# Another order of blocks within one turn of the attention loop

## Chip, cores and metric

The kernel runs on one core of one Trainium2 chip. The metric is the device time of one execution in microseconds; lower is better. Three runs of the kernel before gave 1092.05, 1092.52 and 1094.72.

## What is computed

The input is x, 16 batches of 128 channels by 512 positions, and a context of the same shape. One layer of cross-attention is followed by one layer with a mixture of experts:

```
x = x + xattn(layernorm(x), ctx)      # per batch: q, k, v = 128x128 projections over channels,
                                      # rotary embedding on q and k, 8 heads of 16 channels,
                                      # softmax over 512 positions, output projection
x = x + moe(layernorm(x))             # 2048 tokens of width 512, 32 experts of inner width 192,
                                      # router logits, the best 8 experts, softmax over these 8,
                                      # silu(gate) * up, weighted, down projection, sum
```

## The kernel before

The program is written by hand for each engine, with semaphores between them. It has two parts: the attention with the routing (up to about 534 us of the trace), and a loop over tiles of tokens of one expert (to the end). Only the first part matters here.

The attention is a software pipeline over the 16 batches. In turn `it` the engines work on several batches at different stages: `bl` = it+4 (first normalisation), `bq` = it+3 (projections and rotary embedding of queries and keys), `b1` = it+1 (maxima of the scores, values), `b2` = it (scores, exponentials, averages), `bo` = it-1 (end of the averages, division by the sums, output projection, residual sum), `br` = it-2 (second normalisation, tokens transposed, logits, routing). `batch_turns` (line 274) runs the turns -5 to 19; turns 0 to 14 follow the general order that the change touches, turn 15 and the ones after it have orders of their own.

The names of the work in one general turn:

- TensorE: `s(n)` makes two blocks of scores, n and n+1, side by side (48 or 49 rows each, line 1822); 32 blocks a turn. `m(n)` makes the block of scores for the n-th maximum, also two matmuls side by side (line 1845); 16 a turn. `pv(k)` is the k-th average, eight matmuls in columns of 32, float32 (line 1834); it needs four exponentials. `project` and `project_turned` are the projections of queries and keys and of their turned halves (lines 1520 to 1527, float32; "qr" for the queries and "kr" for the keys), `values` line 1537, `max_rows` the transposes of the maxima (line 1581, first half "mt0", second half "mt1"), `tokens_transposed` line 1586 ("xt"), `logits` line 1606, `output` line 1542, `counts_of` line 1615.
- VectorE: `maximum` (line 1086) reads a block of `m`; `rope` (line 1092) reads a projection; `reciprocal` (line 1120); `highest` and `highest_index` (lines 1149 to 1154) search the best experts in the logits; `choose` (line 1160) compares expert numbers; `weights`, `residual` (line 1231), `read_counts`, `places`, and two statistics (line 1111) before the next turn's first maximum.
- ScalarE: `exponential` (line 813) reads a block of `s`; `read_o` reads the finished averages with their sums out of PSUM, `max_row` the transposed maxima, `high_of_qk` makes the float16 high part of the embedded queries (0) and keys (1), `normal_x`, `normal_x2` normalise, `high_of_x2`, `read_xt`, `read_v`, `turned_half`, `exponentials_of_top`.
- GpSimd: the small steps of both normalisations, products and sums of the rotary embedding (lines 720 and 734), `scale_o` (line 727), low parts (line 606), and the scatter of the routing rows (line 627). Its order is left as it is.
- SyncE issues all other DMAs in an order of its own, which is left as it is: among them the store of the sums (`den_store`), loads of the stacked queries and keys, the store of a row of maxima (`store_mrow`), `store_stack` and the token store.

What sets the order: each engine works strictly in the order of its own `turn` function. PSUM is shared by two rings. The ring of two double banks (`in_v_banks`) is used in turn by m0, the projections, m1 to m8, the logits, m9 to m15, the output and the counts; the ring of three single banks (`in_s_banks`) by the transposed maxima (mt1), s0 to s7, qr, s8 to s11, kr, s12 to s15, xt, s16 to s19, the values, s20 to s25, mt0, s26 to s31. `bank_is_free` (line 296) makes TensorE wait until the tenant two (or three) places back was read. The orders in these two rings are left as they are. Exponentials go to a ring of eight buffers, so e(n) waits for pv(n//4 - 2); the averages have one bank, so pv0 and pv4 wait for `read_o`.

Of the kernel before, what the change touches and what calls it, by code (L numbers as in the profile page):

```python
# [98 lines left out]
def xattn_moe(nc, x, ctx, proj_w, proj_b, value_b, out_w, gate_w, expert_w, const_f, const_h, const_m, out):  # L99
# [26 lines left out]
    with ctxs:  # L126
# [675 lines left out]
        def _(act):  # L802
# [12 lines left out]
            def read_o(b, g):  # L815
                act.wait_ge(pv_mm, b.count(8, 4 * g + 4))

                need(act, on_done, b.count(2, g - 3))
                need(act, den_out, b.count(16, -16))
                copy(o_raw[:, b.slot(2), g, :], ps_o).then_inc(o_read, 1)  # L820

            def max_row(b, half):
                act.wait_ge(mt_mm, b.count(2, half + 1))
                need(act, mrow_in[(b + -1).slot(2)][half], (b + -1).rounds(2, 16, 16))
                copy(mrow[:, half, :], bank(f"mt{half}")[0:16, 0:P], -1.0 / MSCALE).then_inc(mrow_done, 1)
# [15 lines left out]
            def turn(it):  # L841
                bl, bq, b1, b2, bo, br = it + 4, it + 3, it + 1, it, it + -1, it + -2
# [18 lines left out]
                def exponentials_of_top():  # L861
                    act.wait_ge(ntop_done, br.count(1, 1))
                    need(act, rows_done, br.count(3, 0))
                    nc.scalar.activation(ex[:, :], top[:, :], ACT.Exp, bias=ntop[:, 0:1], scale=1.0 / WSCALE, accum_out=exs[:, 0:1]).then_inc(ex_done, 1)

                def normal_x():
                    act.wait_ge(shift1, bl.count(1, 1))
                    need(act, turn_mm, bl.count(2, -1))
                    nc.scalar.activation(xn[:, :], x_in[:, bl.slot(2), :], ACT.Identity, bias=shift[:, 0:1], scale=rstd[:, 0:1]).then_inc(xn_done, 1)


                def exponentials(first, n):
                    if b2.live():
                        for i in range(first, first + n):
                            exponential(b2, i)
# [48 lines left out]
                    return  # L924
                if b2.live():
                    max_row(b2, 1)
                exponentials(0, 6)
                if bo.live():
                    read_o(bo, 1)
                if br.live():  # L930
                    normal_x2(br)
                exponentials(6, 1)
                if br.live():
                    high_of_x2(br)
                exponentials(7, 1)
                if bq.live():
                    turned_half(bq, 0)
                exponentials(8, 4)
# [2 lines left out]
                exponentials(12, 4)  # L941
                if br.live():
                    read_xt()
                exponentials(16, 2)
                if b2.live():
                    read_o(b2, 0)
                exponentials(18, 2)
                if b1.live():
                    read_v(b1)
                exponentials(20, 3)  # L950
                if bq.live():
                    high_of_qk(bq, 0)
                exponentials(23, 1)
                if bq.live():
                    high_of_qk(bq, 1)
                exponentials(24, 2)
                if b1.live():
                    max_row(b1, 0)
                exponentials(26, 3)
                if bl.live():  # L960
                    normal_x()
                exponentials(29, 1)
                if br.live():
                    exponentials_of_top()
                exponentials(30, 2)

            batch_turns(act, turn)

# [533 lines left out]
        def _(pe):  # L1502
# [115 lines left out]
            def turn(it):  # L1618
                bq, b1, b2, bo, br = it + 3, it + 1, it, it + -1, it + -2

                def s(first):
                    if b2.live():
                        for n in (first, first + 1):
                            bank_is_free(pe, it, f"s{n}")
                            scores(b2, n)

                def m(n):
                    if b1.live():
                        bank_is_free(pe, it, f"m{n}")
                        scores_for_maxima(b1, n)  # L1630
# [112 lines left out]
                elif b1.live():  # L1743
                    bank_is_free(pe, it, "qk")
                    constants_into("qk", 2)
                s(6)
                if bq.live():
                    bank_is_free(pe, it, "qr")
                    project_turned(bq, 0)
                elif b1.live():  # L1750
                    bank_is_free(pe, it, "qr")
                    constants_into("qr", 1)
                m(1)
                pv(0)
                s(8)
                m(2)
# [9 lines left out]
                m(4)  # L1766
                s(12)
                pv(2)
                m(5)
                s(14)  # L1770
                if br.live():
                    bank_is_free(pe, it, "xt")
                    tokens_transposed(br)
                m(6)
                m(7)
                s(16)
                pv(3)
                s(18)
                m(8)
# [11 lines left out]
                m(11)  # L1791
                s(24)
                m(12)
                if b1.live():
                    bank_is_free(pe, it, "mt0")
                    max_rows(b1, 0)
                pv(5)
                m(13)
                s(26)
                s(28)  # L1800
                m(14)
                pv(6)
                s(30)
                m(15)
                if bo.live():
                    bank_is_free(pe, it, "y")
                    output(bo)
# [193 lines left out]
```

## Time and profile before

| | |
|---|---|
| median of 3 runs | 1092.52 us (1092.05 to 1094.72) |
| the profiled execution | 1093.14 us, span 1091.3 us |
| granted TensorE clock, mean | 0.966 |
| busy: TensorE, VectorE, ScalarE, GpSimd | 999.5, 701.7, 771.1, 747.1 us |
| 256 maxima on VectorE | 303.9 us, 1222 ns each |
| 512 exponentials on ScalarE | 278.6 us, 603 ns each |

Busy time is that in which an engine executes; it says nothing of why it is idle at other times. The ends of matmuls are modelled, and neighbouring instructions overlap a little at both ends, so the distance between two starts is the better measure of what a step costs. In the rows of a timeline the bracket at the end is idle time just before the instruction and what ended it.

### The profile page before, as it was taken

Reading aid. Unit: us, or ns where it says so; the run is one execution under the profiler, and the core shown is the slowest. Engines: PE = TensorE matmul, PEld = TensorE weight load, DVE = VectorE, ACT = ScalarE, POOL = GpSimd, SP = SyncE. Lnnn points to the kernel's source line nnn. Section 1 sums busy time; section 2 is a strip of 40 time slices with the busy share of each in tenths; the row PEclk is TensorE's granted clock in tenths of the full one; section 3 lists DMA queues with packets and bytes.
Section 4 is the critical chain, followed back from the end, with each engine's and each line's share of the span. In section 5 each row is a group of like instructions: output and inputs, shape, how many; then the busy total and the mean of one; then the engine's idle time right before and its main releaser. Section 6 shows DMA issues by size and latency. Waiting matters only on the chain.

```text
span 1091.3 us, 29745 instructions
## 1 busy us (share of the span) xinstructions
PE 999.5 (92%) x7228; PEld 478.8 (44%) x7229; DVE 701.7 (64%) x1349; ACT 771.1 (71%) x1791; POOL 747.1 (68%) x675
## 2 busy tenths in 40 slices
PE   6689999999999999993499999999999999999995
PEld 2222222222222222231366666666666666666662
DVE  4778899999999988886354555453553554553521
ACT  2278888888888887781367667767677776677673
POOL 5434577777777774457467777777777777777774
PEclk9599999999999999996699999999999999999998
DMA  5524444444344333320588789898789898889673
GB/s 169 159 70 123 139 130 129 126 132 120 118 126 130 119 109 115 98 96 22 173 217 215 212 204 241 216 216 219 198 201 238 215 223 213 218 194 233 119 144 58
DMA packets 88948, 174.56 MB, mean 160 GB/s; under 512 B 23754, under 2 KB 40698, under 8 KB 84786
## 3 DMA queue, kind: packets, MB, share of 16 engines
q0 software_dynamic: 38144, 74.53, 32.0%
q1 hardware_dynamic: 50736, 99.26, 28.5%
q8 instruction: 28, 0.46, 0.2%
q14 instruction: 36, 0.29, 0.1%
q10 hardware_dynamic: 4, 0.02, 0.0%
HBM read 117.26 MB, written 61.58 MB: 164 GB/s over the span
## 4 chain that ended last, share of the span: by engine, by line
PE 41%; issue 4%; DVEq 3%; DVE 2%; DMA 1%; ACTq 1%; ACT 1%; POOL 1%; POOLq 0%; SPq 0%
PE ps L1873 22%; PE ps L1881 5%; PE ps L1899 2%; PE ps L1901 2%; PE ps L1903 2%; PE ps L1902 2%; PE ps L1900 2%; DVEq L374 2%; DVE w_lo L1463 1%; PE ps L1889 1%; DVE w_hi L1458 1%; PE ps L1891 1%; PE ps L1890 1%; ACTq L374 1%; POOL expert_rows L627 0%
## 5 line engine op out<-in xcount | busy, mean ns | idle before, releaser
L1086 DVE TENSOR_REDUCE mx<-ps 128x2 f32<-128x1024 f32 x256 | 303.9, 1222 | 33.9 <-PE ps L1845 29.9
L1873 PE MATMUL ps<-w_hi,o_raw 128*128 x1184 | 313.5, 327 | 0.0
L787 POOL DMA_INDIRECT out<-v,s_idx x148 | 248.2, 1677 | 94.1 <-ACT g_idx L803 41.5
L813 ACT ACTIVATE pr<-ps 128x512 f32<-128x512 f32 x512 | 278.6, 603 | 45.8 <-PE ps L1822 44.6
L766 POOL DMA_INDIRECT pr<-normalised_tokens,g_idx x150 | 163.0, 1087 | 51.8 <-issue 21.7
L1873 PE MATMUL ps<-w_lo,o_raw 128*128 x592 | 193.4, 327 | 0.0
L803 ACT ACTIVATE o_raw<-ps 128x1024 f16<-128x1024 f16 (+1 forms) x180 | 171.9, 955 | 1.3 <-PE ps L1881 1.1
L627 POOL DMA_INDIRECT expert_rows<-rows,rowi x128 | 129.1, 1008 | 38.3 <-issue 37.3
L1873 PEld LDWEIGHTS ps<-w_hi,o_raw 128*128 128x128 f16 x1184 | 116.1, 98 | 84.5 <-issue 0.7
L1475 DVE SCALAR_TENSOR_TENSOR rope_b<-rope_a,stacks,ps 128x192 f32<-128x192 f32 x148 | 60.6, 410 | 142.8 <-ACT rope_a L973 103.9
L1834 PE MATMUL ps<-pr,v 128*32 128x512 f32 x1024 | 136.4, 605 | 0.4 <-issue 0.3
L1845 PE MATMUL ps<-stacks 48*128 48x512 f16 x512 | 104.5, 394 | 21.2 <-DVE mx L1086 18.1
L1822 PE MATMUL ps<-stacks 49*128 49x512 f16 x512 | 112.3, 386 | 12.5 <-ACT pr L813 11.9
L1881 PE MATMUL ps<-ch,pr 128*128 128x128 f16 x1184 | 91.2, 220 | 23.6 <-DMA pr<-normalised_tokens,stacks 22.0
L1480 DVE TENSOR_TENSOR rope_s<-rope_b,rope_s 128x128 f16<-128x128 f32 x148 | 43.0, 291 | 107.3 <-ACT rope_s L803 107.3
L803 ACT ACTIVATE v<-ps 128x512 f32<-128x512 f32 x164 | 96.7, 590 | 2.1 <-PE ps L1537 1.7
L1881 PEld LDWEIGHTS ps<-ch,pr 128*128 128x128 f16 x1184 | 78.2, 98 | 44.3 <-issue 26.1
L1463 DVE SCALAR_TENSOR_TENSOR w_lo<-stage,w_hi x155 | 95.7, 680 | 0.1
L803 ACT ACTIVATE rope_s<-rope_b 128x192 f16<-128x192 f32 x148 | 54.3, 367 | 51.9 <-DVE rope_b L1475 51.7
L803 ACT ACTIVATE x<-ps 128x384 f16<-128x384 f16 x148 | 72.7, 491 | 21.6 <-PE ps L1891 20.9
L1822 PEld LDWEIGHTS ps<-stacks 49*128 49x128 f16 x512 | 30.2, 93 | 123.1 <-ACT pr L813 74.8
L1458 DVE TENSOR_SCALAR w_hi<-stage x62 | 50.1, 849 | 44.6 <-PE ps L1903 35.4
(177 smaller groups left out, 1476.8 us busy)
## 6 DMA issues: line engine op xcount, KB each, us to landing
stage<-in_expert_w SPq DMA_DIRECT2D x32, 1280.0 KB
stacks<-qk_parts SPq DMA_DIRECT2D x128, 96.0 KB
w_lo<-in_x SPq DMA_DIRECT2D x32, 256.0 KB, 2.9
w_lo<-in_ctx SPq DMA_DIRECT2D x32, 256.0 KB, 5.7
qk_parts<-qk SPq DMA_DIRECT2D x32, 256.0 KB
qk_parts<-qk SPq DMA_DIRECT2D x32, 128.0 KB
out<-x SPq DMA_DIRECT2D x16, 256.0 KB, 4.8
normalised_tokens<-x2s SPq DMA_DIRECT2D x16, 256.0 KB, 2.5
```

Source lines behind the costliest of these rows:

```text
L627: nc.gpsimd.indirect_dma_start(rows_d, bass.IndirectOffsetOnAxis(rowi[:, b.slot(2), k:k + 1], 0), rows[:, b.slot(2), k, :], None).then_inc ...
L766: nc.gpsimd.indirect_dma_start(xg[:, r, :], None, tok_d, bass.IndirectOffsetOnAxis(indices, 0)).then_inc(gathered[r], 16)
L787: nc.gpsimd.indirect_dma_start(out_rows, bass.IndirectOffsetOnAxis(s_idx[:, s.slot(4), 0:1], 0), y_sb[:, s.slot(4), :], None, bounds_check ...
L803: copy = lambda o, i, s=1.0: nc.scalar.activation(o, i, ACT.Copy, scale=s)
L813: nc.scalar.activation(pr[:, n % 8, :], bank(f"s{n}"), ACT.Exp, scale=DH ** -0.5).then_inc(exp_done, 1)
L1086: V.tensor_reduce(mx[:, b.slot(2), at:at + 3:2, tile], bank(f"m{n}"), AXX, ALU.max).then_inc(mx_done, 1)
L1463: lo = V.scalar_tensor_tensor(w_lo[:, bass.ds(at_slot + at, LO_PIECE)], stage[:, bass.ds(at_src + at, LO_PIECE)], WSCALE, w_hi[:, bass.ds( ...
L1822: mm(bank(f"s{n}"), k_st[rows_of, b.slot(2), p, sc * P:(sc + 1) * P], q_st[rows_of, b.slot(2), p, :], start=True, stop=True).then_inc(s2_m ...
L1834: last = mm(ps_o[2 * DH * i:2 * DH * (i + 1), :], v1[:, b.slot(2), k % NSC, head, :], pr[:, (4 * k + i) % 8, :], start=(k % NSC == 0), sto ...
L1845: last = mm(bank(f"m{n}")[:, side, :], q_st[rows_of, b.slot(2), p, i * P:(i + 1) * P], k_st[rows_of, b.slot(2), p, :], start=True, stop=True)
L1873: last = mm(ps[:, s.slot(2), 0:2 * INTER], xt[:, s.slot(2), at:at + P], w[:, cols], start=(m == 0), stop=(m == 3 * KT - 1))
L1881: last = nc.tensor.transpose(ps[:, 2 + s.slot(2), :].bitcast(F16)[:, n * P:(n + 1) * P], xg[:, s.slot(GROUP), n * P:(n + 1) * P], ident)
```

## The change

Only the general turn is touched, on TensorE and on ScalarE. No instruction is added or taken away.

```diff
 (ScalarE, turn)
-                exponentials(0, 6)
+                exponentials(0, 4)
                 if bo.live():
                     read_o(bo, 1)
+                exponentials(4, 2)
                 if br.live():
                     normal_x2(br)
-                exponentials(6, 1)
                 if br.live():
                     high_of_x2(br)
-                exponentials(7, 1)
+                exponentials(6, 2)
                 if bq.live():
                     turned_half(bq, 0)
...
-                exponentials(16, 2)
+                exponentials(16, 4)
                 if b2.live():
                     read_o(b2, 0)
-                exponentials(18, 2)
                 if b1.live():
                     read_v(b1)
-                exponentials(20, 3)
+                exponentials(20, 2)
                 if bq.live():
                     high_of_qk(bq, 0)
-                exponentials(23, 1)
+                exponentials(22, 4)
+                if br.live():
+                    exponentials_of_top()
+                if b1.live():
+                    max_row(b1, 0)
+                exponentials(26, 4)
+                if bl.live():
+                    normal_x()
+                exponentials(30, 1)
                 if bq.live():
                     high_of_qk(bq, 1)
-                exponentials(24, 2)
-                if b1.live():
-                    max_row(b1, 0)
-                exponentials(26, 3)
-                if bl.live():
-                    normal_x()
-                exponentials(29, 1)
-                if br.live():
-                    exponentials_of_top()
-                exponentials(30, 2)
+                exponentials(31, 1)
 (TensorE, turn)
                 s(6)
+                m(1)
                 if bq.live():
                     bank_is_free(pe, it, "qr")
                     project_turned(bq, 0)
...
-                m(1)
                 pv(0)
...
                 pv(2)
+                s(14)
                 m(5)
-                s(14)
+                m(6)
                 if br.live():
                     bank_is_free(pe, it, "xt")
                     tokens_transposed(br)
-                m(6)
+                s(16)
                 m(7)
-                s(16)
                 pv(3)
...
                 m(12)
+                pv(5)
                 if b1.live():
                     bank_is_free(pe, it, "mt0")
                     max_rows(b1, 0)
-                pv(5)
+                s(26)
                 m(13)
-                s(26)
                 s(28)
                 m(14)
                 pv(6)
+                m(15)
                 s(30)
-                m(15)
                 if bo.live():
                     bank_is_free(pe, it, "y")
                     output(bo)
```

## Rows read from the trace of the kernel before

**Rows 1.** Stretches: start:end, us, busy of each engine, PEclk, DMA share, GB/s
```profile
105.99:133.71 27.72, 26.27 (x188) 7.97 (x186) 24.44 (x33) 23.86 (x47) 15.62 (x20) 1.00 0.45 136
...
216.82:244.53 27.71, 26.29 (x194) 8.03 (x190) 25.44 (x39) 23.84 (x47) 21.40 (x24) 1.00 0.44 134
```
**Rows 2.** Timeline, TensorE, the turn from 216.82: start, us, engine, line, waits
```profile
219.42 0.39 PE L1822 MATMUL ps<-stacks 49*128 49x512 f16 x1 [0.25 <-ACT pr L813]
...
230.73 0.39 PE L1845 MATMUL ps<-stacks 48*128 48x512 f16 x2 [0.23 <-DVE mx L1086]
...
237.41 0.39 PE L1845 MATMUL ps<-stacks 48*128 48x512 f16 x2 [0.23 <-DVE mx L1086]
...
240.23 0.39 PE L1822 MATMUL ps<-stacks 49*128 49x512 f16 x1 [0.47 <-ACT pr L813]
```
**Rows 3.** The same timeline, steps of TensorE without a wait
```profile
219.74 1.12 PE L1520 MATMUL ps<-xn,pw 128*128 128x512 f32 x2
...
221.65 0.39 PE L1822 MATMUL ps<-stacks 49*128 49x512 f16 x2
221.97 1.12 PE L1525 MATMUL ps<-xn,pw 128*128 128x512 f32 x2
223.03 0.39 PE L1845 MATMUL ps<-stacks 48*128 48x512 f16 x2
223.35 1.06 PE L1834 MATMUL ps<-pr,v 128*32 128x512 f32 x8
224.35 0.39 PE L1822 MATMUL ps<-stacks 49*128 49x512 f16 x2
...
229.02 0.39 PE L1845 MATMUL ps<-stacks 48*128 48x512 f16 x2
229.24 0.38 PE L1822 MATMUL ps<-stacks 49*128 49x512 f16 x2
...
237.73 0.28 PE L1581 MATMUL ps<-ident,mx 128*16 128x128 f32 x1
237.94 1.06 PE L1834 MATMUL ps<-pr,v 128*32 128x512 f32 x8
...
242.30 1.98 PE L1542 MATMUL ps<-o_n,ow 128*128 128x512 f32 x4
```
**Rows 4.** Timeline, VectorE, the same turn
```profile
220.97 1.23 DVE L1086 TENSOR_REDUCE mx<-ps 128x2 f32<-128x1024 f32 x1
...
223.46 1.23 DVE L1086 TENSOR_REDUCE mx<-ps 128x2 f32<-128x1024 f32 x1
225.00 1.23 DVE L1086 TENSOR_REDUCE mx<-ps 128x2 f32<-128x1024 f32 x1 [0.31 <-PE ps L1845]
...
229.45 4.69 DVE L1086 TENSOR_REDUCE mx<-ps 128x2 f32<-128x1024 f32 x4
234.40 0.20 DVE L1149 MAX8 top<-ps 128x8 f32<-128x32 f32 x1 [0.26 <-PE ps L1606]
...
236.14 2.35 DVE L1086 TENSOR_REDUCE mx<-ps 128x2 f32<-128x1024 f32 x2
...
242.41 1.23 DVE L1086 TENSOR_REDUCE mx<-ps 128x2 f32<-128x1024 f32 x1 [0.31 <-PE ps L1845]
243.55 0.41 DVE L1160 TENSOR_TENSOR chosen<-cf,topi 128x256 f16<-128x256 f32 x1
...
244.41 0.68 DVE L1231 TENSOR_TENSOR x<-ps,w_lo 128x512 f32<-128x512 f32 x1
```
**Rows 5.** Timeline, ScalarE, the same turn
```profile
222.93 0.61 ACT L803 ACTIVATE x2s<-xn 128x512 f16<-128x512 f32 x1
...
239.58 1.57 ACT L813 ACTIVATE pr<-ps 128x512 f32<-128x512 f32 x3 [0.70 <-PE ps L1822]
```
**Rows 6.** Timeline, GpSimd, the same turn
```profile
223.62 1.17 POOL L606 TENSOR_TENSOR x2s<-xn,x2s 128x512 f16<-128x512 f32 x1 [0.39 <-ACT x2s L803]
...
241.54 1.16 POOL L606 TENSOR_TENSOR qk<-rope_s,qk 128x512 f16<-128x512 f32 x1
```

## The prediction

> **What bounds the kernel now.** I first read busy time in stretches [rows 1], one stretch per turn of the attention loop. From 105.99 to 466.28 thirteen turns take 27.71 us each on average (the first and the fifth are shown), at a granted TensorE clock of 1.00. In the fifth TensorE is busy for 26.3 us, VectorE in 25.4, ScalarE in 23.8, GpSimd in 21. No engine is full, so the turn is set by a chain that hops between engines. The change touches nothing after the last turn.
>
> Next the timeline of one turn, from 216.82; all offsets below are us after that start. I call the pairs of score blocks s0 to s30, the blocks for the maxima m0 to m15, their readings on VectorE M0 to M15, the exponentials e0 to e31, the averages pv0 to pv7. TensorE stands still in five places, of which four are shown [rows 2]: before s5 (offset 2.60, for e2), m7 (13.91, for M5), m12 (20.59, for M10) and s29 (23.41, for e26); m10 waits for the search of the top experts as m7 and m12 do. Pairs otherwise follow at 0.22 [rows 3]; so s5 is late by 0.63, m7, m10 and m12 by 0.4 each, s29 by 0.85: 2.7 us, which leaves 25.0 us of TensorE's own work. VectorE stands still before M2 (offset 8.18, where M1's start plus 1.14 is 7.78) and in the same way before M3, M4, the search and M15 [rows 4], 2.0 us together: its work is 25.7 us. So 2.0 us a turn is the most that any order can win (26 us in all).
>
> Which waits matter? I follow the chain back from the turn's end. The residual sum (27.59) starts 2.00 after M15 (25.59), and M15 starts 0.42 after m15 (25.17). From the residual sum to the next M0 is 4.27 of VectorE's work in a row (27.59 to 31.86). The block m15 goes back over pv6, m14 and s29 to e26, whose start is 0.65 before s29 [rows 2, 5], then to s26, m12, M10 and so on to M5 and m4. Of the waits, s5 and the first block of the turn are off it: the project block that follows s5 only has to be there before M0 is through.
>
> **The change, part by part.** Durations are taken from the same rows: from a pair to a pair 0.22 to 0.23; from a pair to another kind 0.32; an average 1.00; one turned projection 1.06 when a pair follows [rows 3]; a maximum 0.42 after its block (229.02 to 229.45), the next piece of VectorE 1.14 later (242.41 to 243.55); the block that needs its bank 1.28 after the reading's start (229.45 to 230.73, 236.14 to 237.41) [rows 2, 4].
>
> 1. *m1 ahead of the turned projection of the queries (qr).* Before: s6 at 4.83, qr 5.15, m1 6.21, pv0 6.53. The block m1 needs the bank that M0 reads (M0 at 4.15), so it can't start before 5.43, 0.38 later than TensorE would get there. Behind it stand qr (5.75) and pv0. The join qr to pv0 isn't in the trace: it lies between half of the two projections in a row (1.91/2 = 0.95) and 1.06 [rows 3]. I take 1.00, pv0 at 6.75: 0.22 later than now. M1 itself was ready at 6.64 on both sides (M0, two rope sums, then M1), so the earlier m1 wins nothing on VectorE.
> The Trainium skill (TensorEngine Tiling, Key Properties) says that a change of tiling mode drains TensorE; by it qr to pv0 still pays a drain and would cost the 1.06. That would put 0.06 on every turn. The trace agrees that a change of kind costs 0.10 (0.32 against 0.22).
>
> 2. *s14 ahead of m5, and m6 ahead of the token transposes.* All between pv0 and pv2 keeps its order, so pv2 is at 11.42 (was 11.20). Then s14 12.42 and m5 12.65 (was 12.20 [rows 3]). M5 starts at 13.07 (was 12.63): this is 0.22 from part 1 and 0.22 from the s14 put in front. The moved transposes hide: m7 waits for M5 till 14.35 anyhow, and s17, which now waits for e15 till about 13.98, hides in the same wait. From m7 to M10 nothing changes, but this stretch has two rails. TensorE's rail (m7, pv3, s18, values, logits) is at +0.44; VectorE's was idle for 0.35 before the search (17.58, [rows 4]) and is so no gate. m7 to logits is now 0.23 shorter, as s16 has moved ahead of m7 into the wait; so the logits and the search behind them are at +0.21, 17.79. So M10 is at 19.53, m12 at 20.80 (was 20.59): +0.21.
>
> 3. *pv5 ahead of the transpose of the first maxima; s26 ahead of m13.* Before m12, transpose, pv5, m13, s26: s26 at 22.34, 1.75 after m12. Now m12, pv5 (0.31), transpose (1.00), s26 (0.21): 1.52 after m12, so s26 at 22.32. The join pv5 to transpose isn't shown; it lies between 0.90 and 1.06 (an average's 1.00 less or plus a change of kind), I take 1.00. The reading of this transpose (ScalarE, about 22.4 to 22.7) now ends just when e26 can start (22.74). So s29 comes at 23.39, m14 at 23.61, as before. The +0.21 is made good here. The row of maxima leaves SyncE's queue 0.6 later; it is not needed before the next turn's s0, over 3 us on.
>
> 4. *m15 ahead of s30.* pv6 at 23.92, m15 at 24.92 instead of 25.17, M15 at 25.34 instead of 25.59. But the residual sum needs the output block too. That starts at 25.46 (was 25.48) and the residual needs 2.03 from there (242.30 to 244.41 is 2.11 with M15 as the gate; 1.98 is its own length [rows 3, 4]). So the residual starts at 27.49, not at 27.34. Won: 0.10.
>
> 5. *ScalarE's order.* The reading of the averages moves ahead of e4 and e5; it starts 0.95 earlier, as pv7 was long done. The store of the sums gets ahead, but the reciprocal stands behind M4 on VectorE and had no wait: nothing won. e4 is needed only at 4.83 minus 0.65. The high part of the second normalisation now directly follows it and waits for its own input some 0.2; e6 shifts from 5.63 to about 6.35, needed by s8 at 7.75: hidden. The high part of the keys moves from 20.33 to 26.05, behind e30. GpSimd's low part of them starts 0.69 after it (222.93 to 223.62 [rows 5, 6]), at 26.7 instead of 24.72, and queued behind it are two row scatters, two stack stores and the token store. GpSimd is done about 30.4, the next turn wants it at 31.0: hidden, with 0.6 to spare. The top exponentials go 3 us earlier; VectorE, which takes them up behind the comparison (26.73), had no wait there.
>
> Sum: the next M0 at 27.49 + 4.27 = 31.76, and the next turn's start at 27.69; M0 is then at offset 4.07, 0.08 earlier than I began with. As m1 and all behind it hang on M0, the steady turn is 27.69 - 0.08 = 27.61, against 27.70: **0.09 us shorter**. Thirteen steady turns [rows 1] give 1.2 us; the first two, with parts missing, nothing I can price. The profiled execution took 1093.14 (span 1091.3, 1.84 around it): 1091.9 by the sum. The median of before is 0.62 below that execution, so the forecast is 1092.5 - 1.2 = **1091.3 us**. The open joins (-0.05/+0.06, -0.10/+0.06) and latencies read to 0.03 make -0.18/+0.15 a turn: 1089.0 to 1093.5 on its own.
>
> **Rivals.**
> *The joins are cheap and the output is not the gate* (27%). If qr to pv0 costs 0.90, the transpose after pv5 0.90, and the residual sum follows M15, a turn is 27.3 to 27.4: 0.35 less, 4.6 us, 1087.9. For it: VectorE's rail has the room. Against: the output block is measured at 1.98.
> *TensorE loses more in the first half than it gets back* (15%). m1's wait for M0 and the s14 in front of m5 put 0.44 on M5. If e26 is held up by the late reading of the maxima's transpose (margin 0.07), part 3 gives back nothing: a turn is 27.70 + 0.21 = 27.9, 1095.3. It decides as soon as that reading ends after 22.8.
> *GpSimd is in the way of the comparison* (8%). The comparison (243.55, both inputs in SBUF, 0.41 long [rows 4]) now starts about 0.26 before GpSimd's low part of the keys, which lasts 1.16 [rows 6]; the two never overlap in this trace. Should the low part start first and hold the comparison back, it would wait till 27.8 instead of 26.4, the residual sum starts at about 28.7, 1.2 late, in some 11 turns: 13 us, 1105. It decides if M15 is 0.26 late against s30. The Trainium skill (SBUF — State Buffer, Who interferes with whom) speaks for it: a VectorE instruction with two SBUF inputs contends with a GpSimd instruction that reads SBUF, and the first to start wins; no row here shows it.
> *The orders don't matter* since each engine waits for the same chain: 1092.5; it lies inside the forecast's range.
>
> **The chances.** Forecast 50%, the others 27, 15, 8. A change under 0.3% (3.3 us) is no change to this measurement. The forecast's range is nearly all within that; the first rival is mostly beyond; of the second only half. Faster 0.32, the same 0.46, slower 0.22. The range 1086.0 to 1097.0 leaves out the third rival and tails.
>
> **What would show it.** A steady turn of 27.61 between transposes of the second maxima; m1 waiting for M0 at 5.4; M5 0.4 later in the turn; waits at m7, m12 and s29 still there; M15 earlier, the residual sum not; GpSimd's low part right behind the comparison's start. A turn under 27.45 or over 27.85 makes me wrong; a comparison or a product of chosen and place that starts late while GpSimd is busy names the third rival.

## The result, and the profile after

The changed kernel takes 1100.20 us (median of 6 runs, 1098.25 to 1103.26), the kernel before 1092.71 beside it (6 runs, 1091.71 to 1094.72): a ratio of 1.0068, 95% interval [1.0055, 1.0081]. The forecast was 1091.3 with a range up to 1097.0, so it missed both the sign and the range. The profiled execution took 1098.71 (span 1096.9, granted clock 0.967).

The loss lies in the attention loop. Between transposes of the second maxima the turns of before were 29.37, 26.97, 27.72, and then 27.70 each (one 27.85). After the change they are 28.73, 27.04, 27.39, 28.25, 28.25, 28.51, 27.98, 28.24, 28.24, 28.25, 30.22, 27.74, 29.10, 27.56, 27.37. The last of these transposes starts at 472.32 instead of 466.28: 6.0 us later, of 5.6 in the span.

The same view as [rows 1], two turns of after:

```profile
217.62:245.60 27.98, 26.63 (x193) 8.30 (x189) 25.72 (x39) 24.25 (x47) 20.84 (x23) 1.00 0.42 126
245.60:273.84 28.24, 26.62 (x192) 8.30 (x189) 25.98 (x39) 24.25 (x47) 21.09 (x24) 1.00 0.43 125
```

In the second of them VectorE is busy 0.54 us longer than in [rows 1] (25.98 against 25.44), with the same instructions. One line grouped by form tells which. First before, then after; the columns are the duration in ns (min/median/max) and the first and last start:

```profile
L1173 DVE TENSOR_SCALAR rows<-ex,exr x16: 233/235/341, 133.3 to 509.2; 128x8 f32<-128x8 f32 x16
```
```profile
L1171 DVE TENSOR_SCALAR rows<-ex,exr x16: 233/936/943, 131.9 to 515.3; 128x8 f32<-128x8 f32 x16
```

This scales the 8 routing weights of each token: 128 by 8 numbers, 0.23 us of work, that now takes 0.94. The timeline of VectorE at the end of the turn from 245.60, the counterpart of the last two of [rows 4]:

```profile
272.65 0.41 DVE L1158 TENSOR_TENSOR chosen<-cf,topi 128x256 f16<-128x256 f32 x1
272.99 0.15 DVE L1170 RECIPROCAL exr<-exs 128x1 f32<-128x1 f32 x1
273.18 0.94 DVE L1171 TENSOR_SCALAR rows<-ex,exr 128x8 f32<-128x8 f32 x1
274.03 0.22 DVE L1172 TENSOR_SCALAR rows<-zero,cf 128x16 uint32<-128x16 f32 x1
274.17 0.68 DVE L1229 TENSOR_TENSOR x<-ps,w_lo 128x512 f32<-128x512 f32 x1
```

GpSimd and ScalarE at the same time (compare [rows 6], where the low part of the keys ran at 241.54, well before the comparison at 243.55):

```profile
270.13 1.28 POOL L727 TENSOR_TENSOR o_n<-o_raw,rcb 128x512 f32<-128x512 f32 x1
272.91 1.17 POOL L606 TENSOR_TENSOR qk<-rope_s,qk 128x512 f16<-128x512 f32 x1 [1.51 <-ACT qk L803]
...
272.22 0.62 ACT L803 ACTIVATE qk<-rope_s 128x512 f16<-128x512 f32 x1
```

ScalarE's high part of the keys (272.22) releases GpSimd's low part at 272.91. VectorE's comparison had started 0.26 earlier and runs undisturbed; the scaling comes in the middle and ends at 274.12, when GpSimd's instruction (272.91 + 1.17 = 274.08) is through. The residual sum stands behind it.

In the turn from 330.33 (30.22 us) it was worse. VectorE, GpSimd and TensorE there:

```profile
353.85 3.62 DVE L1084 TENSOR_REDUCE mx<-ps 128x2 f32<-128x1024 f32 x3
357.38 1.15 DVE L1158 TENSOR_TENSOR chosen<-cf,topi 128x256 f16<-128x256 f32 x1
358.46 0.15 DVE L1170 RECIPROCAL exr<-exs 128x1 f32<-128x1 f32 x1
358.65 0.93 DVE L1171 TENSOR_SCALAR rows<-ex,exr 128x8 f32<-128x8 f32 x1
...
360.35 0.69 DVE L1229 TENSOR_TENSOR x<-ps,w_lo 128x512 f32<-128x512 f32 x1 [0.64 <-PE ps L1540]
...
354.64 1.28 POOL L727 TENSOR_TENSOR o_n<-o_raw,rcb 128x512 f32<-128x512 f32 x1 [2.94 <-DMA rcb<-reciprocals]
355.88 1.16 POOL L606 TENSOR_TENSOR qk<-rope_s,qk 128x512 f16<-128x512 f32 x1
356.99 1.26 POOL L727 TENSOR_TENSOR o_n<-o_raw,rcb 128x512 f32<-128x512 f32 x1
358.21 1.34 POOL L606 TENSOR_TENSOR qk<-rope_s,qk 128x512 f16<-128x512 f32 x1
...
358.36 1.95 PE L1540 MATMUL ps<-o_n,ow 128*128 128x512 f32 x4 [1.94 <-DVE mx L1084]
```

The load of the reciprocals came 2.94 us late, GpSimd's chain with it, and now the comparison itself is held (1.15 instead of 0.41) and the output block waits 1.94. The bracket puts that down to VectorE's maximum, whose last one ended at 357.47 at the latest (353.85 + 3.62), 0.9 before; what ended it is GpSimd's second product (356.99 + 1.26 = 358.25). The residual sum (360.35) waits 0.64 for the output, so in this turn the late products set the length and the held instructions of VectorE do not. Each kernel has one traced execution; this one took 1098.71, 1.5 under its kernel's median.

### The profile page after: what moved, and what is told of

It reads as the page before. It is cut to its first block, busy times and chain, and to the rows that moved or that the text cites. A ratio compares the mean times of both kernels' runs of the same rounds, so it can differ in the third digit from the quotient of the medians.

```text
span 1096.9 us, 29745 instructions
## 1 busy us (share of the span) xinstructions
PE 1004.5 (92%) x7228; PEld 482.1 (44%) x7229; DVE 707.6 (65%) x1349; ACT 776.4 (71%) x1791; POOL 746.1 (68%) x675
## 4 chain that ended last, share of the span: by engine, by line
PE 42%; issue 3%; DVEq 2%; DVE 1%; DMA 1%; ACTq 1%; POOL 1%; ACT 0%; POOLq 0%; SPq 0%
PE ps L1871 23%; PE ps L1879 5%; PE ps L1897 2%; PE ps L1899 2%; PE ps L1901 2%; PE ps L1900 2%; PE ps L1898 2%; DVEq L374 1%; PE ps L1887 1%; PE ps L1889 1%; PE ps L1888 1%; DVE w_lo L1461 1%; DVE w_hi L1456 1%; ACTq L374 0%; DMA out<-v,s_idx 0%
## 5 line engine op out<-in xcount | busy, mean ns | idle before, releaser
L1820 PE MATMUL ps<-stacks 49*128 49x512 f16 x512 | 119.9, 388 | 10.3 <-ACT pr L813 9.3
L1820 PEld LDWEIGHTS ps<-stacks 49*128 49x128 f16 x512 | 32.1, 93 | 129.6 <-ACT pr L813 65.8
L1871 PEld LDWEIGHTS ps<-w_lo,o_raw 128*128 128x128 f16 x592 | 58.0, 98 | 45.9 <-issue 0.3
```

The costliest lines, as they stand in the source:

```text
L1820: mm(bank(f"s{n}"), k_st[rows_of, b.slot(2), p, sc * P:(sc + 1) * P], q_st[rows_of, b.slot(2), p, :], start=True, stop=True).then_inc(s2_m ...
L1871: last = mm(ps[:, s.slot(2), 0:2 * INTER], xt[:, s.slot(2), at:at + P], w[:, cols], start=(m == 0), stop=(m == 3 * KT - 1))
```

## The experiments

In the first three batches (e, n) the kernel before took 1125 to 1136 us; in the last two (p, s, q) 1093, as in the forecast. A ratio is against before in the same batch and on the same chip. The e runs were on two chips (e1 to e4, e5 to e8), and the n runs came later on the second of these: the kernel before took 1125.35 there beside e5 to e8 and 1135.69 beside n1 to n4. The p, s and q runs share a third chip. In the expectations theory A is that GpSimd's late low part of the keys, holding VectorE, is the cause; the rival, by whatever letter, is that TensorE's order has a price of its own.

**Moving the high part of the keys, both ways.** On the changed kernel e1 puts it back (as do e5, q1); its edit is shown. On the kernel before e2 moves it alone, from behind e23 to behind e30:

```diff
-                exponentials(22, 4)
+                exponentials(22, 2)
+                if bq.live():
+                    high_of_qk(bq, 1)
+                exponentials(24, 2)
...
-                exponentials(30, 1)
-                if bq.live():
-                    high_of_qk(bq, 1)
-                exponentials(31, 1)
+                exponentials(30, 2)
```

> The changed kernel with one edit: ScalarE's high part of the keys back behind e23, where it was before. Theory A (port): GpSimd's low part of the keys holds VectorE's scaling of the routing weights (0.23 us before, 0.94 us after); with the high part early the low part ends before the comparison, the scaling is 0.23 again, and a steady turn falls from 28.25 to 27.6 to 27.75 us (28.25 less 0.52 that the held scaling puts behind the output's end, or less 0.71 if the output is no gate). Over 12 turns 6 to 8 us: 1091.5 to 1094 us, level with the kernel before (1092.7). Theory B (TensorE's order): the loss comes from m1 waiting for M0 and s14 ahead of m5; the turn stays at 28.0 or more and the time at 1097 or more.

> The kernel before with one edit: the high part of the keys behind e30. Theory A: e30 starts at offset 25.7, so the high part at 26.2 and GpSimd's low part at 26.8 to 28.0; VectorE's scaling at 27.26 is held till 28.0, it lasts about 0.95 us, the residual sum starts 0.7 late, the turn is 28.3 to 28.4, and the time 1092.7 + 12 x 0.7 = 1100 to 1102 us. Theory B: the kernel before keeps its turn of 27.70 and its time of 1092.7, since GpSimd has 0.6 us to spare.

e1: 1136.49 against 1125.48, 1.0100 [1.0065, 1.0134]; e2: 1127.32, 1.0009 [0.9988, 1.0030]. The scaling did as theory A says: 0.23 in e1, 0.94 in e2. VectorE and GpSimd in e2:

```profile
248.83 0.94 DVE L1173 TENSOR_SCALAR rows<-ex,exr 128x8 f32<-128x8 f32 x1
249.82 0.68 DVE L1231 TENSOR_TENSOR x<-ps,w_lo 128x512 f32<-128x512 f32 x1
...
248.46 1.29 POOL L606 TENSOR_TENSOR qk<-rope_s,qk 128x512 f16<-128x512 f32 x1 [2.15 <-ACT qk L803]
```

Four turns of e2 are 28.14 to 28.16, 0.45 over the 27.70 of before; four others are 29.6, and no trace of the kernel before was taken on this chip, so the 0.45 is a comparison across chips. In the whole time it doesn't show: theory A asked for 7 to 9 us more, e2 is 1.8 above before (interval -1.4 to +3.4). And e1's time did not come back: its turns are mostly 30.2 to 31.3 on this chip. The held instruction stood; that it was the loss did not, there.

**The scaling ahead of the last maximum** (on the changed kernel):

```diff
-                maxima(9, 7)
+                maxima(9, 6)
                 if br.live():
+                    weights(br, link)
+                maxima(15, 1)
+                if br.live():
                     choose(br)
-                    weights(br, link)
```

> The changed kernel with one edit on VectorE: the routing weights ahead of the last maximum, behind M14, where GpSimd waits for ScalarE. Their exponentials are ready by offset 22.4 in the changed order. Theory A: scaling 0.23 us, the comparison directly before the residual sum, GpSimd's low part meets nothing that needs its port (the comparison starts 0.2 us before it); a steady turn is 27.6 to 27.75, the time 1091.5 to 1094 us. Theory B: 1097 or more.

1148.65, 1.0213 [1.0178, 1.0248]. Slower yet: the scaling is out of GpSimd's way and the comparison is put in it.

```profile
289.09 0.23 DVE L1171 TENSOR_SCALAR rows<-ex,exr 128x8 f32<-128x8 f32 x1
289.23 0.23 DVE L1172 TENSOR_SCALAR rows<-zero,cf 128x16 uint32<-128x16 f32 x1
289.36 1.22 DVE L1084 TENSOR_REDUCE mx<-ps 128x2 f32<-128x1024 f32 x1
290.50 1.35 DVE L1158 TENSOR_TENSOR chosen<-cf,topi 128x256 f16<-128x256 f32 x1
...
290.42 1.15 POOL L606 TENSOR_TENSOR qk<-rope_s,qk 128x512 f16<-128x512 f32 x1 [5.01 <-ACT qk L803]
```

**GpSimd's low part in halves** (changed kernel; two subtractions of 256 columns):

```diff
+                if w == 1:
+                    sub(qk[:, 2 * w + LO, 0:T // 2], rope_s[:, w, 0:T // 2], ...)
+                    sub(qk[:, 2 * w + LO, T // 2:T], rope_s[:, w, T // 2:T], ...)
+                    return
```

> The changed kernel with one edit on GpSimd: the low part of the keys as two subtractions of 256 columns instead of one of 512. Theory A says that VectorE's scaling waits for the end of the GpSimd instruction that runs when it wants to start, so it now waits for the first half only: it lasts 0.4 to 0.6 us instead of 0.94, and about 0.4 us a turn come back. If instead the two share the port's bandwidth, or GpSimd's being busy at all is what counts, it stays at 0.9 and more.

1139.31, 1.0113 [1.0068, 1.0157]. The scaling takes 0.45: it waits for the end of the GpSimd instruction that is under way, not for the row of them. The next VectorE instruction (L1176, 0.23 elsewhere) then takes 0.72, to 255.04, when the second half is through (253.70 + 1.31 = 255.01).

```profile
253.44 0.41 DVE L1162 TENSOR_TENSOR chosen<-cf,topi 128x256 f16<-128x256 f32 x1
...
253.96 0.45 DVE L1175 TENSOR_SCALAR rows<-ex,exr 128x8 f32<-128x8 f32 x1
254.32 0.72 DVE L1176 TENSOR_SCALAR rows<-zero,cf 128x16 uint32<-128x16 f32 x1
254.96 0.68 DVE L1233 TENSOR_TENSOR x<-ps,w_lo 128x512 f32<-128x512 f32 x1
...
253.70 1.31 POOL L606 TENSOR_TENSOR qk<-rope_s,qk 128x256 f16<-128x256 f32 x2 [3.96 <-ACT qk L807]
```

From the comparison's start to the residual sum's it is 1.52, as in the changed kernel (272.65 to 274.17): the 0.4 us a turn that the expectation hoped for did not come back, since each half held one instruction.

**TensorE's order with ScalarE as before** (e4, e6), **e1 again** (e5), **e1 with the reciprocal of the sums one maximum earlier** (e8):

```diff
 (e4, e6: the changed TensorE turn on the kernel before; e8, VectorE:)
-                maxima(1, 4)
+                maxima(1, 3)
                 if bo.live():
                     reciprocal(bo)
-                maxima(5, 4)
+                maxima(4, 5)
```

> TensorE's order of the changed kernel with ScalarE's order of the kernel before. Theory A: no held scaling, so 27.6 to 27.9 a turn, 1091 to 1095 us; the transpose of the maxima is read by ScalarE where it was before, behind e25. Theory B: this is where the loss is: a turn of 28.2 and 1098 us or more.

> TensorE's order of the changed kernel with ScalarE's order of the kernel before, once more. Theory A, where the transposes are read 0.66 us after their start: scaling 0.23 us, 27.6 to 27.9 a turn, total within 3 us of the kernel before. Theory B: 28.2 a turn and 6 us more.

> The same edit as in the first run (high part of the keys back behind e23), once more. There TensorE's transposes of the tokens ended 1.2 us later than in the two traces the study began with, in every turn, and so did the logits in half of them; the kernel before was 1125 us there. Theory A (port), on a chip where the transposes take 0.66 us from start to reading: scaling 0.23 us, a steady turn of 27.6 to 27.75 us, total within 2 us of the kernel before. Theory B (TensorE's order itself loses): 28.0 or more a turn and at least 4 us more than the kernel before. If the chip is again one where before needs 1125 us: turns of 30 us as in the first run.

> The changed kernel with the high part of the keys behind e23 and, on VectorE, the reciprocal behind M3 instead of M4. The reciprocals then come back from memory about 1.2 us earlier, so GpSimd's products no longer wait for them (0.8 us a turn in the changed kernel's trace, 2.9 and 1.8 in two turns that became 2.0 and 0.9 us longer). Theory A: as e5, without those two long turns: 27.5 to 27.7 a turn, 0 to 3 us below the kernel before. Theory B: 28.0 or more.

e4 1139.05, 1.0123 [1.0096, 1.0151]; e6 1137.61, 1.0112 [1.0068, 1.0156]; e5 1138.82, 1.0113 [1.0081, 1.0145]; e8 1134.75, 1.0086 [1.0061, 1.0111]. So on these chips TensorE's order costs over 1% with ScalarE's left alone. That is a second cost, beside theory A. e8 takes away the waits for the reciprocals in the steady turns, which stay at 30.2: those waits aren't it.

**Both kernels again, part 2 alone, and part 2 undone** (n3 on the kernel before; n4 undoes it in e1):

```diff
 (n3; n4 is the reverse, in e1)
                 pv(2)
+                s(14)
                 m(5)
-                s(14)
+                m(6)
                 if br.live():
                     bank_is_free(pe, it, "xt")
                     tokens_transposed(br)
-                m(6)
-                m(7)
                 s(16)
+                m(7)
```

> The changed kernel, nothing edited, to have its trace on the same chip as the other experiments. In eight runs the kernel before needed 1125 us, and in TensorE's new order the transposes of the tokens were ready 1.2 us late in every turn from turn 3 on. Theory C (dense spots): where many short TensorE instructions stand together (8 transposes with 8 weight loads, 12 logits with 12 loads) this chip runs late, and the new order, with m5, m6 and the transposes behind one another, makes that worse. It expects 1.2 us late transposes here too and, with the held scaling (0.94 us) on top, a time of 1138 to 1145 us. Theory A alone (port) expects it 6 us above the experiment with the high part of the keys early (1136 to 1139): 1142 to 1145. If it is at 1138 or less, the held scaling is hidden by the late transposes on this chip.

> The kernel before, nothing edited, for its trace on this chip. It must come out at the same time as the kernel before beside it (ratio 1.00). Theory C: its transposes are read at the usual 1.07 us after their start (ScalarE's own pace) in turns 3 to 12, the logits are late in some turns, turns are 27.7 to 29 us, and the stage between the attention and the loop of the experts is longer than in the first trace (39 us there).

> The kernel before with one edit on TensorE: s14, m5, m6, transposes, s16, m7 instead of m5, s14, transposes, m6, m7, s16. Theory C: the transposes come 1.2 us late in every turn from turn 3 on, a steady turn is 29.5 to 30.5 us and the time 1135 us or more on a chip where before is at 1125; on a chip where before is at 1093, no such delay and 1092 to 1095. The rival (the delay comes from m1 standing ahead of the projection, or from pv5): this kernel stays at the time of before.

> The changed kernel with the high part of the keys behind e23 and with this one part of TensorE's order (s14, m5, m6, transposes, s16, m7) put back as before. Theory C: no late transposes, a steady turn of 27.5 to 28.5 us, the time level with before or up to 4 us below. The rival: turns of 30 us and 1135 us or more as in the experiment that leaves this part in.

Before was at 1135.69 in this batch. n1 1155.14, 1.0191 [1.0150, 1.0232], nearly three times the first result's loss; n2 1137.04, 1.0013 [0.9986, 1.0041]; n3 1142.55, 1.0041 [1.0016, 1.0066]; n4 1142.52, 1.0071 [1.0038, 1.0104]. The traces show where the extra goes. TensorE, VectorE and ScalarE in n1:

```profile
240.09 0.62 PE L1584 MATMUL ps<-ch,x2s 128*128 128x128 f16 x8
245.09 0.46 PE L1604 MATMUL ps<-gws,x2t 128*128 128x32 f16 x12
247.75 0.39 PE L1843 MATMUL ps<-stacks 48*128 48x512 f16 x2 [1.66 <-issue]
...
247.13 0.20 DVE L1147 MAX8 top<-ps 128x8 f32<-128x32 f32 x1 [1.70 <-PE ps L1604]
...
242.00 1.02 ACT L803 ACTIVATE x2t<-ps 128x1024 f16<-128x1024 f16 x1 [1.15 <-PE ps L1584]
```

The transposes of tokens started at 240.09 are read at 242.00, 1.91 later, and the logits (245.09) at 247.13, 2.04 later. In the first result's trace of the same kernel these are 0.66 and 0.60. In n2, the kernel before, they are mostly 1.07 and between 0.61 and 1.46 for the first eleven batches of tokens, against 1.07 and 0.60 in the forecast's trace, and its turns are mostly 29.0. The granted clock is 1.00 in the stretch from 170 to 260 of n1. So on these chips the results of the short matmuls reach their readers late, the more so in the new order. Part 2, which stood under suspicion, doesn't account for it: alone (n3) it costs 0.4%, but with it undone (n4) the transposes are still read after mostly 1.4 and the logits after mostly 1.8, the turns are mostly 29.5 to 32.1, and the time is 0.7% above before, where theory C had expected it level.

**Each part alone, on a chip that runs before at 1093.35** (28 runs). p1 is part 1, p3 part 3, p4 part 4, s ScalarE's new order with the keys left behind e23 (lines with `if` and `bank_is_free` are not printed):

```diff
 (p1)
                 s(6)
+                m(1)
                 project_turned(bq, 0)
-                m(1)
                 pv(0)
 (p3)
                 m(12)
+                pv(5)
                 max_rows(b1, 0)
-                pv(5)
-                m(13)
                 s(26)
+                m(13)
 (p4)
+                m(15)
                 s(30)
-                m(15)
```

> The kernel before with part 1 alone (m1 ahead of the turned projection of the queries). Theory A (only the late high part of the keys costs anything) says the weights' scaling stays at 0.23 us and the time is that of before within 0.3%, as pv0's 0.22 is made up at the waits. Theory C (on these chips TensorE's order has a price of its own, because blocks of many short matmuls land late when more dense work stands ahead of them) says the reading of the token transposes stays near 1.07 us after their start, since nothing near them is moved: within 0.3% as well. The prediction's second rival says up to 0.21 us a turn, 1.0025.

> The kernel before with part 3 alone (pv5 ahead of the transpose of the first maxima, s26 ahead of m13). The prediction had it win up to 0.21 us a turn where something upstream is late and nothing otherwise: ratio 0.998 to 1.000. Theory C: the transpose of the maxima is a single matmul, nothing dense is moved, so 1.000. A ratio over 1.003 says that the exponentials behind s26 or the store of the maxima pay for it.

> The kernel before with part 4 alone (m15 ahead of s30). Forecast's step: M15 0.25 us earlier, the residual sum 0.10 earlier: ratio 0.999. A rival: e30 and e31 start later by 0.22, and with them the first pieces of the next turn, so nothing is won or 0.1 lost a turn: 1.000 to 1.001. The scaling of the weights stays at 0.23 us.

> TensorE as before; ScalarE in the changed order but with the high part of the keys behind e23 as before. Theory A: nothing is left that holds VectorE, scaling 0.23 us, 0.998 to 1.002 of before. Theory C: TensorE's order is that of before, so 1.000 as well. If it is slower by over 0.3% then ScalarE's order has a cost beside the keys (the earlier reading of the averages in front of e4, say), and part 5 fails in a second place.

| kernel | us | ratio to before | steady turn |
|---|---|---|---|
| p1 | 1095.49 | 1.0017 [1.0006, 1.0029] | 27.98 (+0.28) |
| p3 | 1090.29 | 0.9966 [0.9953, 0.9980] | 27.48 (-0.22) |
| p4 | 1093.00 | 0.9992 [0.9980, 1.0003] | 27.70 (0.00) |
| s | 1093.36 | 0.9999 [0.9986, 1.0012] | 27.70 (0.00) |

The steady turn is the length that recurs most in the trace to 0.02: in eleven or more turns for p3, p4 and s and in six for p1; further on in nine for q2, four for q1, and five of the changed kernel. TensorE in p1, from its turn's start at 161.23:

```profile
161.23 0.27 PE L1581 MATMUL ps<-ident,mx 128*16 128x128 f32 x1
...
166.66 0.39 PE L1845 MATMUL ps<-stacks 48*128 48x512 f16 x2 [0.21 <-DVE mx L1086]
166.98 1.13 PE L1525 MATMUL ps<-xn,pw 128*128 128x512 f32 x2
168.04 1.07 PE L1834 MATMUL ps<-pr,v 128*32 128x512 f32 x8
```

m1 is at 5.43, as forecast; pv0 at 6.81, 0.28 later than before, and no wait behind takes that up. TensorE in p3:

```profile
214.65 0.27 PE L1581 MATMUL ps<-ident,mx 128*16 128x128 f32 x1
235.23 0.39 PE L1845 MATMUL ps<-stacks 48*128 48x512 f16 x2 [0.23 <-DVE mx L1086]
236.55 0.28 PE L1581 MATMUL ps<-ident,mx 128*16 128x128 f32 x1
237.83 0.39 PE L1822 MATMUL ps<-stacks 49*128 49x512 f16 x1 [0.25 <-ACT pr L813]
242.13 0.27 PE L1581 MATMUL ps<-ident,mx 128*16 128x128 f32 x1
```

m12 stays at 20.58, s29 comes at 23.18 instead of 23.41 [rows 2], with a wait of 0.25 instead of 0.47, and the turn is 27.48. Thirteen such turns make 2.9 us of the 3.06 between the medians. This is the fastest kernel of the study, 0.34% under before.

**The sum of the parts** (q1 is e1 again; q2 also undoes part 1), before at 1092.91:

> The changed kernel with the high part of the keys back behind e23. If this chip runs the kernel before at about 1093, the reading of the token transposes should come 0.66 us after their start as in the changed kernel there, and theory A gives a steady turn of 27.6 to 27.8 (the walk corrected for the held scaling gives 27.61; the measured parts added, 27.70 + 0.28 - 0.22 + 0.00, give 27.76): ratio 0.998 to 1.001. If it runs before at 1125 or more, theory C gives 1.010 again with turns over 30 us. Scaling 0.23 us either way.

> The same with part 1 undone too (m1 back behind the turned projection): TensorE's parts 2, 3 and 4, ScalarE's order with the keys early. By the parts measured alone (part 1 0.28 us a turn, part 3 -0.22, part 4 0.00, ScalarE 0.00) the steady turn is 27.48 if part 2 is free and at most 27.70 if it costs the 0.22 that s14 puts in front of m5: ratio 0.9965 to 1.000, and under that of the kernel beside it. Theory C: where before runs at 1125, part 2 keeps its 0.4 per cent, 1.000 to 1.007.

q1 1095.92, 1.0024 [1.0015, 1.0033], steady turn 27.73 (its traced execution, 1099.62, was the slowest of its eleven). q2 1093.55, 1.0001 [0.9991, 1.0011], steady turn 27.49. TensorE's waits in q1 and then in q2:

```profile
217.19 0.27 PE L1579 MATMUL ps<-ident,mx 128*16 128x128 f32 x1
222.59 0.39 PE L1843 MATMUL ps<-stacks 48*128 48x512 f16 x2 [0.18 <-DVE mx L1084]
...
240.63 0.39 PE L1820 MATMUL ps<-stacks 49*128 49x512 f16 x1 [0.25 <-ACT pr L813]
244.92 0.27 PE L1579 MATMUL ps<-ident,mx 128*16 128x128 f32 x1
```
```profile
215.43 0.27 PE L1579 MATMUL ps<-ident,mx 128*16 128x128 f32 x1
...
238.62 0.39 PE L1820 MATMUL ps<-stacks 49*128 49x512 f16 x1 [0.25 <-ACT pr L813]
242.92 0.27 PE L1579 MATMUL ps<-ident,mx 128*16 128x128 f32 x1
```

So the change splits up in the steady turn: keys late 28.25 - 27.73 = +0.52, part 1 27.73 - 27.49 = +0.24, part 3 -0.22, and 0.01 is left for parts 2 and 4 and the rest of ScalarE's order. These are differences from kernel to kernel, so that they add up to 28.25 - 27.70 = 0.55 proves nothing; what does is that part 1 costs about the same alone (0.28) and in company (0.24), and that q2 and p3 have the same turn. Of the 6.0 us between the traces of after and before, seven such turns make up 3.65 (one is longer, one shorter); the three turns from the eleventh to the thirteenth make 3.96, with waits of 2.94 and 1.84 us for the reciprocals in the first and the third; the rest gives 1.6 back.

The expectation for both ratios was too low, because not all turns are steady ones. q2 has turns of 28.36 and 28.72 and q1 of 31.22 and 28.82, each with a wait of 1.6 to 3.0 us for the load of the reciprocals near it. The 31.22 one in q1, on VectorE and GpSimd:

```profile
355.29 1.13 DVE L1158 TENSOR_TENSOR chosen<-cf,topi 128x256 f16<-128x256 f32 x1
...
352.53 1.27 POOL L727 TENSOR_TENSOR o_n<-o_raw,rcb 128x512 f32<-128x512 f32 x1 [2.95 <-DMA rcb<-reciprocals]
356.10 1.33 POOL L606 TENSOR_TENSOR qk<-rope_s,qk 128x512 f16<-128x512 f32 x1
```

There the low part is late although its input is early: it is queued behind the late products.

In the whole time these turns outweigh the steady ones. q2 has the steady turn of p3, yet takes 1093.55 where p3 takes 1090.29. Part 4 and ScalarE's order cost nothing alone (p4, s), so the 3.3 us belong to part 2 or to parts in company; no run has part 2 alone on this chip.

## Why the prediction was wrong, point by point

**The step that failed is part 5, ScalarE's order**: "GpSimd is done about 30.4, the next turn wants it at 31.0: hidden, with 0.6 to spare". The order in it was right: the comparison starts 0.26 ahead of the low part. Both come 0.6 later than forecast (the low part at 27.31 to 28.48 after the turn's start, said 26.7 to 27.9; the comparison at 27.05). What it left out was that a GpSimd instruction off the path can lengthen a VectorE instruction on the path. It costs 0.71 in the scaling and 0.52 in the turn, since without the hold the residual sum waits for the output (0.21 at 216.99 in q1). The hold is shown by moving this step alone both ways: the scaling is 0.23 with the keys early (e1, e5, q1) and 0.94 with them late (e2). Its price in time rests on the changed kernel (7.5 us above before) against q1 (3.0 above before), 4.5 us, in separate batches that both ran before at 1093; the two were not run side by side there.

**A second term was missing.** With the keys early the time is still 3.0 us over before (q1), where the forecast had 1.2 under. The sum took thirteen steady turns and had nothing for turns in which the reciprocals land late. The steady turn of q1 explains 0.4 of it; its long turns, in the one execution traced, are where the rest stands. Why they come up is open.

**The third rival had the mechanism** with 8%, and named the comparison as its victim with 1.2 us a turn. In the steady turn the comparison wins its 0.26 start, as forecast, and the next VectorE instruction but one is hit instead. The Trainium skill (SBUF — State Buffer, Who interferes with whom), as the prediction drew on it, has the first to start win; the traces agree (comparison first: 0.41; GpSimd first by 0.08 in e3: 1.35), and e7's 0.45 agrees with a hold until the running instruction ends. The same section says of tensor_scalar that it can take the shared port pair as well, if its operands meet certain conditions; that is the form that was hit, and whether this one meets them was not examined. The rule was applied to one instruction where all of VectorE's row behind it, for the 1.17 us of GpSimd's instruction, had to be gone through.

**Part 1**: m1 at 5.4 as said (5.43 alone). pv0 0.28 late, not 0.22: the join of the turned projection and the average is 1.06 (166.98 to 168.04), the upper end of the range. The Trainium skill (TensorEngine Tiling (Array Packing), Key Properties) says that changing the tiling mode drains TensorE and gives no figure; the prediction took the 1.06 for such a join from its rows, and the trace agrees with 1.06 here too. That the earlier m1 "wins nothing on VectorE" was right.

**Part 2**: "+0.21 at m12" came true only as part 1's share: m12 is at 20.84 in q1 and at 20.59 in q2, where part 2 stands without part 1 and M5 is later by 0.21 (12.84). The transposes hide, as the step said. It is free in the steady turn (27.49 in q2, 27.48 in p3); that it is free in the whole time is not shown, as q2 takes 3.3 us more than p3.

**Part 3**: -0.22 measured alone, 0.21 said. It only "made good" what part 1 lost.

**Part 4**: m15 ahead of s30 was to win 0.10. Alone the residual sum does come a little earlier, but the turn is 27.70 as before. It is at 27.50 after the start; in the one turn that the prediction read it was at 27.59, in the turns around it at 27.52 to 27.54, so the win is 0.03 in most turns. The chain was read wrongly there: in the kernel before the turn doesn't close over the residual sum and M0, but over TensorE's own row from the transposes of maxima over s5, m5, the logits, m12, s26 and s29 to the next transposes. p1 and p3 support it: their +0.28 and -0.22 pass to the turn whole. Only with part 1 in place, where m1 waits for M0 (0.21 in p1, 0.18 in q1), can M0 be on the loop; that is read from the waits, no run tests it.

**The sum**: 27.61 was forecast. Without the held scaling it is 27.73 (q1), of the 0.12 between them 0.06 the join in part 1 and 0.05 M0, which starts at 4.12 instead of 4.07. The range on its own was added up a little wide: 13 turns of 0.15 end at 1093.3, not 1093.5. By the steady turn alone part 5 as forecast would have left the time within 0.1% of before; q1 measured 1.0024.

## To carry to other kernels

When an instruction of GpSimd on SBUF moves in time, list every VectorE instruction that will run beside it, short ones too, and price each at the end of the GpSimd one: an idle engine is not a free place. To find the loop that sets a turn, shift one block and see whether the turn shifts by the same amount; a chain read backwards from the last instruction can pass a gate that has slack. Parts of a reordering that win and lose the same amount should be tried one by one: one of the four on TensorE was worth 0.34% by itself. And a forecast made of steady turns needs a look at the turns that aren't: one late load made a turn 2.5 us longer here (30.22 against 27.70).

## What was not expected of the hardware

An instruction of 128 by 8 numbers was held for 0.71 us by one of GpSimd's. The reciprocal (128 by 1, 0.15) at 272.99, which started while the same GpSimd instruction ran, was not held.

The same program in other batches, on other chips, is not only slower (1125 to 1136 against 1093 for the kernel before, and on one chip 1125.35 and later 1135.69) but weighs orders otherwise: the whole change costs 1.9% there and 0.7% here, and e1 1.0 to 1.1% there and 0.24% here. Late results of short matmuls (1.9 and 2.0 us in n1 instead of 0.66 and 0.60) are what the traces show of it. Why they are late stays open; that dense rows of short instructions are supplied late is only argued. Open is, too, why the load of the reciprocals is late by up to 3 us in some turns of after, q1 and q2: its way through DRAM took 10.2 us from the reciprocal to the product in such a turn of q2 (337.77 to 348.00) and 8.7 in one of before (340.01 to 348.69), where the product waited for nothing. In turns of before where it waited the way took up to 9.7 (284.45 to 294.17), with a wait of 1.14 that did not lengthen the turn. No run took the orders behind it apart.
